# Splitting projections into three levels with two engines instead of three, and one wait per one-hot tile

## What is computed

```
x = x + 0.5 * L0_ffn(norm(x));  x = x + L0_attn(norm(x));  x = x + 0.5 * L0_ffn(norm(x))
x = x + 0.5 * L1_ffn(norm(x));  x = x + L1_attn(norm(x));  x = x + 0.5 * L1_ffn(norm(x))

L0_attn: q = x @ Wq.T + bq;  k = x @ Wk.T + bk;  v = x @ Wv.T + bv      # 2 projections that are split
L1_attn: q1, q2, k1, k2 = x @ Wq1, x @ Wq2, x @ Wk1, x @ Wk2;  v = x @ Wv   # 4 projections that are split
L0_ffn:  the 8 best of 64 experts for each token; xe[expert, position] = token; ...
```

## Time and profile before

| | us |
|---|---|
| median of 3 runs | 6747.85 |
| lowest and highest run | 6737.48, 6751.71 |
| the profiled execution | 6750.49 |
| its span in the profile | 6748.4 |
| TensorE busy in the span | 5221.8 (77%) |
| VectorE busy | 3307.6 (49%) |
| ScalarE busy | 2556.6 (38%) |
| GpSimd busy | 1576.2 (23%) |
| granted TensorE clock, mean | 0.88 |

### The profile page before, as it was taken

One profiled execution on the slowest core, in us unless ns is written; L12 is line 12 of the kernel. 1 busy time (PEld: TensorE's weight loads), 2 busy tenths in 40 slices (PEclk: granted clock), 3 DMA queues, 4 the chain that ended last, 5 costly groups with the idle time before them and its releaser, 6 DMA issues. The chain is left out here.

```text
span 6748.4 us, 94042 instructions
## 1 busy us (share of the span) xinstructions
PE 5221.8 (77%) x30108; PEld 2792.5 (41%) x30112; DVE 3307.6 (49%) x4783; ACT 2556.6 (38%) x5006; POOL 1576.2 (23%) x1276
## 2 busy tenths in 40 slices
PE   6566558888787566489968688888888888977997
PEld 3454223333225355248943233333323333344686
DVE  7411646666545621311157566666666666543011
ACT  2311116655561311122221265556555665612221
POOL 2488200000001288333323000000000001002332
PEclk9678769999898687789989699999999999988998
DMA  2476431112103277408945111111111111011498
GB/s 93 114 149 131 144 95 42 42 48 62 56 27 111 74 153 148 115 0 295 315 162 161 47 34 45 52 38 34 46 51 37 34 47 50 16 62 35 160 314 274
DMA packets 454295, 660.14 MB, mean 98 GB/s; under 512 B 97984, under 2 KB 308992, under 8 KB 448672
## 3 DMA queue, kind: packets, MB, share of 16 engines
q1 hardware_dynamic: 383232, 544.50, 25.8%
q0 software_dynamic: 70656, 110.44, 8.1%
HBM read 489.33 MB, written 164.20 MB: 97 GB/s over the span
## 5 line engine op out<-in xcount | busy, mean ns | idle before, releaser
L1670 DVE TENSOR_REDUCE ea_mx<-ea_psA 128x1 f32<-128x1024 f32 (+7 forms) x1280 | 1317.0, 1061 | 691.8 <-PE ea_psA L1535 484.4
L1652 ACT ACTIVATE ea_pr<-ea_psB 128x512 f32<-128x512 f32 (+3 forms) x2560 | 1229.5, 535 | 928.6 <-PE ea_psB L1557 508.1
L1532 PE MATMUL ea_psA<-ea_kx,ea_qx 99*128 99x512 bf16 (+3 forms) x2560 | 728.5, 362 | 284.3 <-DMA ea_kx<-in_c_k 255.0
L1670 DVE TENSOR_REDUCE ba_mx<-ba_psA 128x1 f32<-128x1024 f32 (+7 forms) x640 | 657.2, 1061 | 379.3 <-PE ba_psA L1535 279.9
L1557 PE MATMUL ea_psB<-ea_qx,ea_kx 99*128 99x512 bf16 (+3 forms) x2560 | 782.2, 354 | 29.1 <-issue 21.1
L1652 ACT ACTIVATE ba_pr<-ba_psB 128x512 f32<-128x512 f32 (+3 forms) x1280 | 610.7, 535 | 493.3 <-PE ba_psB L1557 259.4
L1572 PE MATMUL ea_psO<-ea_pr,ea_vx 128*32 128x512 f32 (+3 forms) x5120 | 610.5, 549 | 1.9 <-ACT ea_pr L1652 0.4
L1532 PE MATMUL ba_psA<-ba_kx,ba_qx 108*128 108x512 bf16 (+3 forms) x1280 | 370.5, 368 | 197.9 <-DMA ba_kx<-in_c_k 180.1
L1532 PEld LDWEIGHTS ea_psA<-ea_kx,ea_qx 99*128 99x128 bf16 x2560 | 217.5, 100 | 691.9 <-issue 378.5
L1504 POOL DMA_DIRECT2D ea_qx<-ea_mT x192 | 105.6, 557 | 1540.0 <-DVE ea_mT L1692 1515.8
L1557 PEld LDWEIGHTS ea_psB<-ea_qx,ea_kx 99*128 99x128 bf16 x2560 | 242.3, 99 | 500.9 <-ACT ea_pr L1652 315.0
(11 more groups left out here) (524 smaller groups left out, 8248.3 us busy)
## 6 DMA issues: line engine op xcount, KB each, us to landing
de_wg<-in_L_rg SPq DMA_DIRECT2D x64, 512.0 KB, 4.6
de_wu<-in_L_ru SPq DMA_DIRECT2D x64, 512.0 KB, 5.7
de_wd<-in_L_rd SPq DMA_DIRECT2D x64, 512.0 KB, 7.2
fe_wg<-in_L_rg SPq DMA_DIRECT2D x64, 512.0 KB, 4.6
fe_wu<-in_L_ru SPq DMA_DIRECT2D x64, 512.0 KB, 5.6
fe_wd<-in_L_rd SPq DMA_DIRECT2D x64, 512.0 KB, 7.0
ae_w<-in_L_w SPq DMA_DIRECT2D x64, 384.0 KB, 3.8
ce_w<-in_L_w SPq DMA_DIRECT2D x64, 384.0 KB, 3.5
```

What stands on the lines that cost most here:

```text
L1532: last = nc.tensor.matmul(psA[:, slot, at:at + n], qx[0:KB, s, hh, t * P:(t + 1) * P], kx[0:KB, s, hh, k:k + n], start=True, stop=not diag)
L1652: nc.scalar.activation(pr[:, j % 2, hh, off:BLK], psB[:, exp_slot(n, s), off:BLK], ACT.Exp).then_inc(s_exp, 1)
L1670: v.tensor_reduce(out, src, AX.X, ALU.max).then_inc(s_ar, 1)
```

## The change

In project_phase ScalarE reads each PSUM buffer twice: one activation writes t32 as before, a second one with the same scale and bias writes the first level in bfloat16. The wait for the slot's store stands on ScalarE between the two, and s_t is counted after the second. VectorE's first cast goes; it makes the first remainder, the second level, and now the third level too, and its last step counts s_lo, which releases SP's store and, two units later, ScalarE. GpSimd's program of this phase goes, and the semaphore s_r with it.

In invert_tiles_dve the first four tiles are written out without a wait; from then on each tile waits until the tile four before it is used, where one wait stood ahead of each group of four.

```diff
-    with dve.Fori(0, NT // TU) as i:
-        dve.wait_ge(R["s_oh_used"], i * TU)
+    def tile(t, tt, first):
+        if not first:
+            dve.wait_ge(R["s_oh_used"], t - (TU - 1))
+        own, of_tile = slice(tt * K, (tt + 1) * K), ds(t * K, K)
+        nc.vector.tensor_tensor(R["ohr"][:, own, 0:NCOL], columns_of(NCOL), over(R["cf"][:, of_tile], NCOL),
+                                ALU.is_equal).then_inc(R["s_ohr"], 1)
+        nc.vector.tensor_tensor(R["ohp"][:, own, :], columns_of(P), over(R["pf"][:, of_tile], P),
+                                ALU.is_equal).then_inc(R["s_ohp"], 1)
+
+    for tt in range(TU):
+        tile(tt, tt, True)
+    with dve.Fori(1, NT // TU) as i:
         for tt in range(TU):
-            own, of_tile = slice(tt * K, (tt + 1) * K), ds((i * TU + tt) * K, K)
-            nc.vector.tensor_tensor(R["ohr"][:, own, 0:NCOL], ...
-            nc.vector.tensor_tensor(R["ohp"][:, own, :], ...
+            tile(i * TU + tt, tt, False)
...
                 def scaled(n, b, i, k, m, half, first):
                     act.wait_ge(s_mm, n + 1)
-                    after(act, s_r, n, 2, first)
+                    after(act, s_lo, n, 2, first)
                     a = {} if vbias is None else {"bias": bias[:, 2 * m + half:2 * m + half + 1]}
                     f = ACT.Copy if vbias is None else ACT.Identity
-                    nc.scalar.activation(t32[:, k % 2, :], ps[:, k % 2, :], f, scale=mats[m][2],
+                    nc.scalar.activation(t32[:, k % 2, :], ps[:, k % 2, :], f, scale=mats[m][2], **a)
+
+                    act.wait_ge(s_out[k % NL], ((b * QB + i) * (nu // NL) + k // NL) * 16)
+                    nc.scalar.activation(lev[:, k % NL, 0], ps[:, k % 2, :], f, scale=mats[m][2],
                                          **a).then_inc(s_t, 1)
...
                     dve.wait_ge(s_t, n + 1)
-
-                    dve.wait_ge(s_out[v], ((b * QB + i) * (nu // NL) + k // NL) * 16)
-                    nc.vector.tensor_copy(lev[:, v, 0], t32[:, u, :]).then_inc(s_c, 1)
+                    nc.vector.tensor_tensor(res[:, u, :], t32[:, u, :], lev[:, v, 0], ALU.subtract).then_inc(s_c, 1)
                     dve.wait_ge(s_c, base + n * 2 + 1)
-                    after(dve, s_lo, n, 2, first)
-                    nc.vector.tensor_tensor(res[:, u, :], t32[:, u, :], lev[:, v, 0], ALU.subtract).then_inc(s_c, 1)
+                    nc.vector.tensor_copy(lev[:, v, 1], res[:, u, :]).then_inc(s_c, 1)
                     dve.wait_ge(s_c, base + n * 2 + 2)
-                    nc.vector.tensor_copy(lev[:, v, 1], res[:, u, :]).then_inc(s_r, 1)
+                    nc.vector.tensor_tensor(lev[:, v, 2], res[:, u, :], lev[:, v, 1], ALU.subtract).then_inc(s_lo, 1)
...
-            @block.gpsimd
-            def _(pool):
-                def rest(n, b, i, k, m, half, first):
-                    pool.wait_ge(s_r, n + 1)
-                    nc.gpsimd.tensor_tensor(lev[:, k % NL, 2], res[:, k % 2, :], lev[:, k % NL, 1],
-                                            ALU.subtract).then_inc(s_lo, 1)
-                blocks(pool, rest)
```

More of the change, by code:

```diff
@@ L449, in invert_tiles_dve @@
     columns_of = lambda n: R["iota"][:, 0:n].unsqueeze(1).broadcast_to((P, K, n))
-    with dve.Fori(0, NT // TU) as i:
-        dve.wait_ge(R["s_oh_used"], i * TU)
-        for tt in range(TU):
-            own, of_tile = slice(tt * K, (tt + 1) * K), ds((i * TU + tt) * K, K)
[L454 to L457, removed]
+    def tile(t, tt, first):
[9 more added lines that the diff above has]
+    with dve.Fori(1, NT // TU) as i:
+        for tt in range(TU):
+            tile(i * TU + tt, tt, False)
 def invert_tiles_act(nc, act, R, K, NCOL):
@@ L1109, in project_phase @@
         psV = sc.ps("psV", [P, 2, BLK])
-        s_w, s_vw, s_mm, s_t, s_c, s_r, s_lo, s_vm, s_vs, s_vi = (
-            sc.sem(n) for n in ("w", "vw", "mm", "t", "chain", "r", "lo", "vm", "vs", "vi"))
+        s_w, s_vw, s_mm, s_t, s_c, s_lo, s_vm, s_vs, s_vi = (
+            sc.sem(n) for n in ("w", "vw", "mm", "t", "chain", "lo", "vm", "vs", "vi"))
         s_out = [sc.sem(f"out{u}") for u in range(NL)]
```

## The result

| | before | after |
|---|---|---|
| median of 5 runs each, us | 6741.11 | 6658.36 |
| lowest and highest run | 6733.94, 6751.71 | 6645.62, 6665.03 |
| ratio, 95% interval | | 0.9873 (0.9858 to 0.9889) |
| profiled execution, its span | 6750.49, 6748.4 | 6658.36, 6656.3 |

The change takes 1.3% off. It was forecast as faster, at 6674 us; it brought more than that. The size was missed by 16 us, and the time stands at the very low end of the range (6658).

A forecast was written before the change was run, and what follows sets the result against it. VectorE was taken to bound the projections, partly by waiting for GpSimd, and to stall in the one-hot tiles. Gains of 51.0 and 23.2 us, 74.2 in all, gave 6674 us beside the median 6747.85; range 6658 to 6698.

The forecast's parts named there:

- the base: Whole kernel: starting time before the change, a median of 6747.85 us, from which the gain of 74.2 was taken.
- the loop edges: Loop turns in projections and one-hot tiles: 2.0 us taken off the projections' gain, 0.5 off each routing stage's.
- The bound and the mechanism: Projections: VectorE sets the pace, and some 0.83 of its subtraction's 1.52 us is waiting for GpSimd.
- The unit, 1.81: Projections: VectorE needs 0.73 + 0.47 + 0.61 = 1.81 us a unit afterwards, against 2.373 in ep and 2.397 in bp.
- Before the units: Projections' start: second activation ahead of the first unit costs 0.6 us a phase; bp's second unit waits 0.6 for matmuls.
- GpSimd's 1.26 ... is not a gain of its own: Projections' end: GpSimd's late 1.26 us ran beside the next unit, so its removal adds no further gain.
- The one-hot part: Routing stages: stalls per group of four vanish, 12.1 less 0.5 us each, 23.2 in two; fulfilled waits counted as free.
- A: Projections: ScalarE's slower pass, 0.60 against 0.42, lies on the path and costs 0.18 a unit; 6691 us, chance 0.08.
- B: Routing: the one-hot stage gives nothing back, since something else holds the group rhythm; 6697 us, chance 0.04.
- C: Projections: denser stores land late, near 7.9 us, and eat the rest of the gain; about 6748 us, chance 0.02.
- D: Projections: TensorE's clock falls to 1.2 GHz, 3.44 us a unit; slower, 6826 us, chance 0.03.
- E: Projections: the subtraction's 1.52 us is its own and not GpSimd's doing, 3.47 a unit; 6829 us, chance 0.01.

The follow-up runs named there:

- the part alone: Kernel before with only the one-hot tiles' per-tile wait changed, the projections left as before: 6723.55 us beside 6740.69, ratio 0.9974.

## Why the prediction was right and wrong, point by point

Of the 15.6 us between the forecast and the median of after, 6.7 are the base and the rest is gain that the sum left out: 7.4 by stages, 6.8 in the projections and 0.6 in the routing. The mechanism held; what failed was the base, and in the sum above all the loop edges.

**The bound and the mechanism: right.** VectorE set the pace of the projections, 0.83 of its 1.52 were waiting for GpSimd, and without GpSimd the subtraction takes 0.68. That the waiting is GpSimd's doing is shown twice, by taking GpSimd away and by putting it back with work that nobody needs.

**The unit, 1.81: a little long.** Measured 1.79. Its three instructions came out as assumed; the hand-overs were 0.03 instead of 0.04, and the last subtraction overlapped by 0.08 as taken. Over 96 units 1.9 us.

**The loop edges, 2.0 taken off: the step that failed.** They are not lost a second time. In ep the mean period equals the steady one, 1.79; in bp it is 0.016 more, 0.5 in all, and 0.43 of that is the wait of bp's second unit, which the prediction took off by itself. So the 2.0 weren't paid. The same term was taken off in the one-hot part, 0.5 in each stage (though its own price, 2.0 over 14 edges, makes 1.0 of seven): from 181.71 to 240.75, where the last tile begins, 26 tiles take 59.04, which is 26 x 2.27, with no edge in it. Together 3.0 us of gain that the prediction denied, the largest wrong term of its sum.

What the term stood for can be read in before. At six places in each phase the units fall behind, three times by 0.44 us and three times by 0.15. That is 1.8 a phase; the means gave less, since they hold short periods at the start too (1.65 in ep, 1.82 in bp). At the larger ones GpSimd's instruction comes before the cast, which then takes 1.32 to 1.42 instead of 0.42; in the first of them VectorE had idled for 0.20 that the profile puts down to no wait:

```profile
3538.21 1.15 POOL L1243 TENSOR_TENSOR ep_lev<-ep_res,ep_lev 128x512 bf16<-128x512 f32 x1 [1.09 <-DVE ep_lev L1225]
...
3538.32 1.32 DVE L1220 CAST ep_lev<-ep_t 128x512 bf16<-128x512 f32 x1 [0.20 <-issue]
```

These edges are gone with either half of the change alone: apart from the first and last units of ep, every period is 1.89 to 1.91 with the cast moved and 2.25 to 2.26 with the third level moved. Why is not shown. One reading fits: the turn of the loop passes beside the last instruction of its body and needs more than the 0.43 of the cast that stood last in before, while 0.69, 1.21 or 1.26 stand last in the others. No run tests it by itself. Edges of the old loop are no measure of the new one.

**Before the units: right.** VectorE's first instruction starts 1.12 us behind ScalarE's first activation in ep and 1.29 in bp, where it was 0.63 and 0.72; the second activation cost 0.49 and 0.57, and 0.6 was put. bp's second unit lost 0.43 where 0.6 was put.

**"GpSimd's 1.26 ... is not a gain of its own": doubtful.** The stage of v behind the units was taken as unchanged. From v's first copy to the attention's first load it is 1.7 us shorter in ep (60.5 to 58.8) and 0.3 in bp. In before v's first store was issued at 3654.79, 1.92 us after VectorE's first copy, since SP first had to store the last unit, which waited for GpSimd; in after it is 0.69, as these rows show:

```profile
3578.80 0.69 DVE L1231 TENSOR_TENSOR ep_lev<-ep_res,ep_lev 128x512 bf16<-128x512 f32 x1
3579.41 1.25 DVE L1240 COPY ep_vs<-ep_psV 128x496 f32<-128x496 f32 x2
3580.10 1.15 SPq L1157 DMA_DIRECT2D vd<-ep_vs  x2
```

That looks like the cause, but the third level moved alone gives the same early store (0.7), and v's stage there is 60.7, no shorter than before. In the other kernels whose projections are those of after it lies between 58.7 and 60.0, so part of the 1.7 is chance; what else shortened it stays open. Of the 6.8 us that the projections brought beyond the 51.0, the unit, the edges and the phases' starts explain 4.2 and v 2.0. The rest, 0.6, is the wait for the weights: the first matmul starts 0.45 us sooner in ep and 0.13 in bp after the first load was issued, and this wait differs by as much between profiles of kernels with the same projections.

**The one-hot part: right but for the edges.** 23.2 predicted, 23.8 measured, so 0.6 of the 1.0 for edges came out as gain, with VectorE's new start stretched by GpSimd's last addition, and a fulfilled wait for each tile that costs nothing (a tile is 2.27 as before). SP's store of all_x hid, as said.

**The base.** The forecast was hung on a median of three runs, 6747.85. Five runs gave 6741.11, and the 19 and 13 beside the experiments 6740.69 and 6739.15. 6740.7 less the 81.6 of the stages is 6659; the start was 7 us too high, and the sum of terms 7.4 too small. Below the forecast the range held 16 us: 7 for the spread of the runs, and 9 for a last subtraction as quick as a cast, which didn't come (693 ns). The two errors have the same sign and used up all of it. That the 6658.36 still lies inside is luck; the four later runs of the same kernel, at 6647.4, don't.

**The rivals.** A: the pair on ScalarE is 1.09 us long in ep and 1.26 in bp, 0.1 under what was costed, and the pass that is 0.17 slower there is off the path; VectorE waited 2.2 us for ScalarE in ep, not 0.18 a unit. The rule that simple arithmetic belongs on VectorE (the Trainium skill, "ScalarE: Activation LUTs", "Rules for kernel authors"), carried over to a cast, which its row doesn't list, would have kept the cast where it was. The cast's move is worth 0.46 of the 0.57 us a unit: here, where VectorE is the bound and ScalarE was idle for three quarters of the stage, the slower engine is the cheaper one. B: out, by the part alone. C: out, 2.5 us to landing. D: out, a granted clock of 0.99 and 1.00 with TensorE busy 115.98 of 117 us. E: out, 684 ns.

## What to carry to other kernels

Cost a move by the engine that is full, not by the instruction's price: 0.59 on an idle engine beat 0.42 on the bound. When an engine's work is taken away because it stands in another's way, count what the other has to do instead; here 0.83 of waiting was given for 0.69 of work and a hand-over, and the move beside it was worth four times as much. And start a forecast from as many runs of before as there are: when the gain is 1%, a median of three can be off by a tenth of it.

## What the runs showed of the hardware that was not expected

- Of the instructions of VectorE and GpSimd that met in these rows the one that started later did most of the waiting, and a lead of 0.16 us decided it: GpSimd's subtraction 1.26 or 1.53, VectorE's 1.52 or 0.68, and a plain cast 1.26 to 1.37 instead of 0.43.
- A float16 comparison of 128 x 1024 takes 1.21 us where one operand repeats an element 128 times in a row, and 0.68 with the 8 choices innermost and a stored table as the other operand. The two were changed together; which of them brings it was not run apart.
- Read with a step of 8 float16 elements (16 bytes), 128 x 1024 take ScalarE 2179 ns instead of 1147, and TensorE's moving operand of 128 columns 414 ns instead of 314 at a granted clock of 0.50; TensorE's weights with the same step cost the matmul nothing (311) and their loads 15 ns (166 instead of 151). The Trainium skill, "SBUF — State Buffer", section "Door 1: The DMA port swizzle", says that SBUF has lines of 16 bytes and that each access that goes on to a new line pays a penalty. The first two numbers agree with it; it doesn't say that weights are spared, and there the measurement decides.
